# Moving twelve small matrix products from the end of one expert stage into the next, and the routing steps around them

## The reference, cut to what matters

```python
# fourth: mixture of 8 experts, 2 per token (also run as the sixth)
gate_logits = xt @ Wg.T + bg
w, idx = top_k(gate_logits, 2); w = softmax(w)
h = relu(xt @ W1[e].T + b1[e]); y = h @ W2[e].T + b2[e]      # per expert e
out = sum over the two chosen experts of w * y
x = x + 0.5 * out
# fifth: attention over 256 fixed source rows, 16 heads of 64
v = (value_embedding @ Wv + bv).reshape(256, 16, 64)
ctx = softmax(qn @ kn.T / 8) @ v;   h = ctx @ Wo + bo
```

## Time and profile before

| | |
|---|---|
| three runs, us | 1052.39, 1052.88, 1051.32 (median 1052.39) |
| profiled execution, us | 1052.39 |
| its span, first to last instruction, us | 1050.6 |
| mean granted TensorE clock | 0.827 |
| D1 on TensorE | about 555 to 606 us |
| D2 on TensorE | about 606 to 651 us |
| S2 on TensorE | from 651.25 us |

### The profile page before, as it was taken

The page is one execution under the profiler, slowest core; times in us unless marked ns, Lnnn a source line. Parts: engine busy times, 40 slices in busy tenths (PEclk is TensorE's granted clock), DMA queues, the critical chain, the costliest instruction groups (busy, mean ns, idle before and its releaser), DMA issues.

```text
span 1050.6 us, 18271 instructions
## 1 busy us (share of the span) xinstructions
PE 946.2 (90%) x5092; PEld 725.6 (69%) x5092; DVE 789.6 (75%) x3092; ACT 576.1 (55%) x1313; POOL 459.1 (44%) x538
## 2 busy tenths in 40 slices
PE   5999988998889898966999999989999999997994
PEld 2668866877677676755996677866666666667863
DVE  5865899999999999995556963547878786866234
ACT  3547654554544454523764554867767677652541
POOL 2620079887568767845003762013602040132034
PEclk9999965555555555555999999999999999998998
DMA  9976422000700000022675315630100000005852
GB/s 305 315 230 200 129 72 100 14 13 11 102 2 13 8 1 9 14 75 82 203 215 168 100 49 161 185 104 21 42 1 1 1 22 1 1 24 168 248 161 73
DMA packets 63444, 95.66 MB, mean 91 GB/s; under 512 B 12128, under 2 KB 41968, under 8 KB 63216
## 3 DMA queue, kind: packets, MB, share of 16 engines
q1 hardware_dynamic: 46256, 71.94, 23.6%
q0 software_dynamic: 6144, 12.60, 4.2%
q10 hardware_dynamic: 10944, 9.97, 2.8%
HBM read 69.94 MB, written 30.83 MB: 96 GB/s over the span
## 4 chain that ended last, share of the span: by engine, by line
PE 45%; DVE 26%; issue 3%; ACT 3%; POOL 3%; DMA 1%; SPq 0%; POOLq 0%; ACTq 0%; DVEq 0%
DVE vb L1745 10%; PE bank L798 10%; DVE sg L1747 9%; PE bank L407 6%; PE bank L783 5%; PE bank L420 4%; PE bank L364 4%; PE bank L376 3%; PE bank L773 3%; PE bank L767 2%; PE bank L552 1%; PE bank L395 1%; POOL yg L2101 1%; PE bank L321 1%; PE bank L759 1%
## 5 line engine op out<-in xcount | busy, mean ns | idle before, releaser
L2101 POOL DMA_INDIRECT yg<-ys,posg x96 | 95.2, 992 | 140.7 <-issue 70.1
L1770 POOL TENSOR_SCALAR vb<-sS,vb 128x256 f32<-128x256 f32 x126 | 115.7, 930 | 67.7 <-DVE vb L1745 62.4
L1745 DVE MAX8 vb<-sg 128x8 f32<-128x256 f32 x384 | 142.6, 411 | 0.0
L1144 ACT ACTIVATE hb<-sS,negm 128x256 f32<-128x256 f32 x128 | 58.0, 502 | 115.3 <-POOL negm L2117 114.0
L2085 POOL DMA_INDIRECT xsc<-xnS,posu x96 | 96.3, 1003 | 53.3 <-DVE posu L1516 26.8
L407 PE MATMUL bank<-xbT,ws 128*128 128x256 f32 x456 | 114.3, 388 | 0.0
L552 PEld LDWEIGHTS bank<-kn,qn 128*128 128x128 f32 x512 | 112.0, 320 | 1.5 <-ACT qn L1150 1.5
L552 PE MATMUL bank<-kn,qn 128*128 128x17 f32 x512 | 106.5, 349 | 1.0 <-ACT qn L1150 1.0
L1747 DVE MATCH_REPLACE8 sg<-vb,sg 128x256 f32<-128x256 f32 x256 | 102.5, 406 | 0.0
L1776 POOL TENSOR_TENSOR hb<-vb,hb 128x512 f32<-128x512 f32 x63 | 79.9, 1269 | 31.5 <-ACT hb L1144 24.5
L364 PE MATMUL bank<-xnT,ws 128*128 128x512 f32 x192 | 92.7, 611 | 0.8 <-ACT xnT L958 0.8
(11 more groups left out here) (225 smaller groups left out, 1910.5 us busy)
## 6 DMA issues: line engine op xcount, KB each, us to landing
ws<-tab_m SPq DMA_DIRECT2D x46, 450.0 KB, 4.1
ws<-tab_m SPq DMA_DIRECT2D x54, 321.0 KB, 3.5
xb<-xsc SPq DMA_DIRECT2D x76, 128.0 KB, 3.2
ys<-ysb ACTq DMA_DIRECT2D x76, 128.0 KB, 3.4
xsc<-qn SPq DMA_DIRECT2D x3, 2048.0 KB, 16.3
pk<-packed SPq DMA_DIRECT2D x1, 3209.0 KB, 11.0
tab_m<-packed SPq DMA_DIRECT2D x5, 512.0 KB
ws<-packed SPq DMA_DIRECT2D x8, 256.0 KB, 4.4
```

The costliest lines, as they stand in the source:

```text
L1745: e.max(m8s[:, m:m + 8], s).then_inc(A["tk"], 1)
L1770: i = e.tensor_scalar(msk[:, n * S:n * S + S], sS[:, s:s + S], m[:, n, TOPK - 1:TOPK], None, ALU.is_ge)
L2101: e.indirect_dma_start(yg[:, y:y + D], None, ys[:, :], at(posg[g.p], g.order[t], k)).then_inc(s_g[t % GY], 16)
```

## The change

The twelve value steps all go into D2; the two that stood at steps 16 and 17 of D1 go to steps 1 and 2 of D2, and the later ones are spread anew. `D2.m` is transposed on TensorE before the last `pe_dense_second` of D1. In D2 the routing of p2 starts one step earlier on TensorE, but its place on VectorE comes one step later; that of p3 comes one to two steps later: its rank on TensorE goes from step 9 to step 11, and the transpose of the D2 weights from 10 to 11. On VectorE the four combines of D1's step 15 become one at step 14, one at 15 and two at 16. GpSimd scatters three tiles' halves, then five, then the rest, where it was four, three and the rest.

```diff
-        VALUES_D1 = {16: (0, 1), 17: (1, 1)}
-        VALUES_D2 = {4: (2, 0), 6: (3, 1), 7: (4, 1), 10: (5, 1), 11: (6, 1), 12: (7, 1), 13: (8, 1), 14: (9, 1), 15: (10, 1),
-                     16: (11, 1)}
+        VALUES_D2 = {1: (0, 0), 2: (1, 0), 3: (2, 0), 4: (3, 0), 6: (4, 0), 8: (5, 1), 9: (6, 1), 10: (7, 1),
+                     13: (8, 1), 14: (9, 1), 15: (10, 1), 16: (11, 1)}
...
             if n == 0:
                 e.wait_ge(s_ld[4], 16)
-                e.wait_ge(M["off"], S2.parts[0].nth)
-            elif n == 2:
                 e.wait_ge(R["lg"], D2.m.q + 1)
-            elif n == 3:
+            elif n == 5:
                 e.wait_ge(M["off"], S2.parts[1].nth)
-            elif n == 5:
+            elif n == 8:
                 e.wait_ge(M["off"], S2.parts[2].nth)
...
             elif j == 16:
-                pe_values(e, *VALUES_D1[j])
-            elif j == 17:
                 e.wait_ge(F["b2x"], D1.i + 1)
                 pe_T(e, D2.m)
-                pe_values(e, *VALUES_D1[j])
+            elif j == 17:
                 pe_logits(e, D2.m)
...
-            if j == 3:
-                values_read(e, 2)
+            if j == 2:
+                e.wait_ge(M["off"], p1.nth)
                 pe_T(e, p2)
-            elif j == 4:
+            elif j == 3:
                 pe_logits(e, p2)
             elif j == 5:
                 pe_rank_part(e, p2)
-            elif j == 6:
-                values_read(e, 3)
+            elif j == 7:
+                values_read(e, 5)
                 pe_T(e, p3)
-            elif j == 7:
+            elif j == 9:
                 pe_logits(e, p3)
-            elif j == 9:
-                values_read(e, 5)
+            elif j == 11:
+                e.wait_ge(M["off"], p2.nth)
+                values_read(e, 8)
                 pe_rank_part(e, p3)
-            elif j == 10:
-                e.wait_ge(R["lg"], p3.q + 1)
                 pe_combT(e, D2)
-            elif j == 11:
+            elif j == 12:
                 pe_b2(e, D2)
...
-        COMBINE_D1 = {5: (0,), 6: (1,), 7: (2,), 8: (3,), 9: (4,), 10: (5,), 11: (6,), 12: (7,), 15: (8, 9, 10, 11)}
+        COMBINE_D1 = {5: (0,), 6: (1,), 7: (2,), 8: (3,), 9: (4,), 10: (5,), 11: (6,), 12: (7,), 14: (8,), 15: (9,), 16: (10, 11)}
...
-            elif j == 15:
+            elif j == 16:
                 dve_stats(e, p2)
+            elif j == 18:
+                dve_top2(e, D2.m)
...
             if j == 0:
                 dve_stats(e, p3)
-                dve_top2(e, D2.m)
...
-            elif j == 7:
+            elif j == 9:
                 dve_top2(e, p3)
-            elif j == 8:
+            elif j == 10:
                 dve_choice(e, p3)
-            elif j == 9:
+            elif j == 11:
                 dve_place_part(e, p3)
                 dve_place_end(e, S2)
...
-            pool_scatter(e, S2, 0, 4)
+            pool_scatter(e, S2, 0, 3)
             pool_rstd(e, S2.parts[1])
-            pool_scatter(e, S2, 4, 7)
+            pool_scatter(e, S2, 3, 2 * CT)
             pool_rstd(e, S2.parts[2])
-            pool_scatter(e, S2, 7)
+            pool_scatter(e, S2, 2 * CT)
```

More of the change, by code:

```diff
@@ L727, in values_read, with pe_values @@
             after(e, C["VOe"], n - 4)
-        def pe_values(e, n, b):
+        def pe_values(e, j):
+            n, b = VALUES_D2[j]
             if n == 0:
                 e.wait_ge(s_ld[4], 16)
-                e.wait_ge(M["off"], S2.parts[0].nth)
-            elif n == 2:
                 e.wait_ge(R["lg"], D2.m.q + 1)
-            elif n == 3:
+            elif n == 5:
                 e.wait_ge(M["off"], S2.parts[1].nth)
-            elif n == 5:
+            elif n == 8:
                 e.wait_ge(M["off"], S2.parts[2].nth)
@@ L887, in pe_beside_d2 @@
                 pe_rank_part(e, p2)
-            elif j == 6:
-                values_read(e, 3)
+            elif j == 7:
+                values_read(e, 5)
                 pe_T(e, p3)
-            elif j == 7:
+            elif j == 9:
                 pe_logits(e, p3)
-            elif j == 9:
-                values_read(e, 5)
+            elif j == 11:
+                e.wait_ge(M["off"], p2.nth)
+                values_read(e, 8)
                 pe_rank_part(e, p3)
-            elif j == 10:
-                e.wait_ge(R["lg"], p3.q + 1)
                 pe_combT(e, D2)
-            elif j == 11:
+            elif j == 12:
                 pe_b2(e, D2)
             if j in VALUES_D2:
-                pe_values(e, *VALUES_D2[j])
+                pe_values(e, j)
         def pe_beside_s2(e, n):
@@ L945, in tensor_program @@
             pe_dense(e, D2, pe_beside_d2)
-            values_read(e, len(VALUES_D1) + len(VALUES_D2))
+            values_read(e, len(VALUES_D2))
             pe_blocks(e, S2, pe_beside_s2)
@@ L1264, in act_a1_key, with act_values @@
                 act_a1_sq(e, key_step(j, 1))
-        def act_values(e, n, b):
+        def act_values(e, j):
+            n, b = VALUES_D2[j]
             if n == 0:
@@ L1324, in act_beside_d1 @@
                 act_xn(e, D2.m)
-                act_values(e, *VALUES_D1[16])
                 act_xnT(e, D2.m)
-                act_values(e, *VALUES_D1[17])
         def act_beside_d2(e, j):
@@ L1332, in act_beside_d2 @@
                 act_xn(e, p2)
-            elif j == 2:
+            if j in VALUES_D2:
+                act_values(e, j)
+            if j == 2:
+                act_th(e, D2.m)
                 act_xnT(e, p2)
[L1335 to L1340, removed]
+            elif j == 4:
                 act_th(e, p2)
             elif j == 6:
+                act_xn(e, p3)
+            elif j == 7:
                 act_xnT(e, p3)
-            elif j == 8:
+            elif j == 10:
                 act_th(e, p3)
-            elif j == 10:
+            elif j == 11:
                 act_combT(e, D2)
@@ L1381, in scalar_program @@
             act_dense(e, D2, act_beside_d2)
-            act_values(e, *VALUES_D2[2 * E])
+            act_values(e, 2 * E)
             e.preload_act_table_set("natural_log_exp_and_others")
@@ L2002, in dve_beside_d2 @@
                 dve_choice(e, p2)
+            elif j == 5:
                 dve_place_part(e, p2)
-            elif j == 7:
+            elif j == 9:
                 dve_top2(e, p3)
-            elif j == 8:
+            elif j == 10:
                 dve_choice(e, p3)
-            elif j == 9:
+            elif j == 11:
                 dve_place_part(e, p3)
```

## The result

Four runs of the changed kernel took 1057.31 to 1060.13 us, median 1058.88 us; four runs of the kernel before, on the same chip, 1051.32 to 1052.88 us, median 1052.62 us. The ratio is 1.0058, with a 95% interval of 1.0044 to 1.0072: slower by about 6 us. Forecast were 1056.3 us, in a range from 1052.6 to 1058.4 us. The record has nine more executions of the changed kernel, the profiled one among them, without runs of the kernel before set beside them; all thirteen lie between 1056.54 and 1060.50 us, with a median of 1058.00 us.

What follows compares the result with a forecast made beforehand. TensorE, busy 90% of the span, was taken as the bound, with VectorE pacing D1's end. D1's gain -0.65, value steps +1.74, new D2 waits +1.15 and clock +1.7 gave +3.94 us on 1052.39: 1056.3 us, range 1052.6 to 1058.4.

Steps and rivals of the forecast that it cites:

- the term of 1.7 us for the fall of the clock: Behind TensorE's longer pause at D1's end the clock falls to half rate, losing 1.7 us of full-speed work.
- The upper bound of the term: A second clock fall, for the 0.8 us wait in D2, would cost another 1.7 us; not expected.
- x(5) 0.65 us later: End of D1: tile 8's combine ahead of x(5) on VectorE delays it and the last second product, to 602.39.
- Transpose of `D2.m` inside the pause, at about 600.9: End of D1: the transpose falls into TensorE's wait before the last second product, taking 0.44 us off the path.
- VT0 and VT1 cost 1.74 us in D2: Early D2: the two moved value steps add 2 x 0.87 us on TensorE, which had no gap there.
- Waits of 0.8 and 0.25 us in D2: Early D2: TensorE waits 0.8 us for p2's normalised rows before its transpose, 0.25 us before VT1 for bank 0.
- VO7's 0.78 us stays: In D2, TensorE's existing 0.78 us wait before VO7, for the eviction of VO6, remains.
- The first block: S2's first block lands at 651.9 to 653.0, before TensorE comes at 653.49, so it stays hidden; cover 0.5 us.
- What follows S2 moves as a whole: After S2 the work keeps its order and shifts together; nothing counted for it.
- the clock stays up: Rival, end of D1: the transpose in the pause is enough to hold the clock; +2.24 us, 1054.6 us, chance 0.20.
- waits are covered: Rival, D1's end and early D2: x(5) not later, no new waits, clock stays; +0.44 us, 1052.8 us, chance 0.10.
- The other side: Rival, D1's end: x(5) done before TensorE's transpose, all three old waits saved, 2.83 us; 1049.6 us, chance 0.10.

Runs made afterwards that it cites:

- combines back: The changed kernel with the four combines of tiles 8 to 11 back at VectorE's step 15, behind x(5): 1054.45 us, ratio 1.0032.
- two value steps back: The changed kernel with VT0 and VT1 back at steps 16 and 17 of D1, all else as changed: 1054.42 us, ratio 1.0025.
- useless work in D1: The changed kernel with four extra matmuls, results never read, in TensorE's pause before the transpose of D2.m: 1055.38 us against 1052.33 us, ratio 1.0035.
- logits behind wide products: The changed kernel with the logits of D2.m moved behind the first two products of D2: 1056.45 us, ratio 1.0043.
- value steps alone, second run: The kernel before with only VT0 and VT1 moved from D1 to steps 1 and 2 of D2, repeated on another chip: 1057.26 us against 1051.63 us.
- x(5) early, second run: The kernel before with x(5) ahead of p1's place, VT0 and VO7 on bank 0, repeated on another chip: 1049.76 us against 1051.63 us, ratio 0.9978.
- the experiment with useless work: The kernel before with useless matmuls in its two other long TensorE pauses, second attention and D3: 1052.52 us against 1051.63 us, ratio 1.0008.

## Why the prediction was right and wrong

The direction was right, and so was the kind of mechanism: a fall of the clock behind the longer pause. The size was not, and the median fell 0.5 us outside the range.

The step that failed is the term of 1.7 us for the fall of the clock in the sum -0.65 + 1.74 + 1.15 + 1.7. It measured 4.4 us: the clock was at half rate for 10.2 us and not for 3.4. The upper bound of the term, two times 1.7 us, lay below it too, and its reason did not occur: the wait of 0.41 us that was left brought no fall. With the rows, the sum is about 2.5 us without the clock, less 0.2 us of a shorter wait, plus 4.4: 6.7 us, as S2's start shows.

I had read the length from one pause of one trace and taken it for a constant. It is none, even with the same work on both sides. Eight profiles have this pause near 950 us, of 3.86 to 3.88 us for `zacc`, with the same 32 instructions behind it:

| kernel | 32 instructions start | clock falls, about | low clock, us |
|---|---|---|---|
| before | 953.22 | 954.1 | 3.4 |
| changed | 959.70 | 960.1 | 3.4 |
| combines back | 955.77 | 956.0 | 3.4 |
| two value steps back | 954.74 | 956.0 | 3.4 |
| useless work in D1 | 956.64 | 955.6 | 6.8 |
| logits behind wide products | 957.37 | 956.3 | 6.8 |
| value steps alone, second run | 960.03 | 958.3 | 6.8 |
| x(5) early, second run | 950.04 | 948.9 | 6.8 |

Two rows of the fifth:

```profile
955.00:956.00 1.00, 0.00 (x0) 0.82 0.19 66
...
956.64 6.61 PE L796 MATMUL bank<-VO,sS 128*128 128x129 f32 x32 [3.88 <-DVE zacc L1877]
```

Where the clock fell after TensorE had gone back to work it stayed low for 3.4 us, where it fell before that for 6.8. The same pause has both, so its length and the work behind it do not fix the cost. Nor is the moment of the fall a rule for D1: with the value steps alone it fell behind the restart and stayed low for 10.2 us. The trace of before held a warning. For 100 us in another stage the clock is near half rate, with TensorE busy for 91 of them:

```profile
200.00:300.00 100.00, 91.35 (x385) 0.52 0.21 34
```

With this row in view the term would have had a wider bound. That the forecast missed by so little is partly luck: the term was short by 2.7 us, and the time grew by less than S2's start moved.

- *x(5) 0.65 us later*: x(5) started 0.66 us later, the last second product at 602.40 where 602.39 was forecast. The kernel with the combines back undid this.
- *Transpose of `D2.m` inside the pause, at about 600.9*: 600.93. That it would not keep the clock up was called likelier than not, and so it was in all profiles with the transpose alone.
- *VT0 and VT1 cost 1.74 us in D2*: not measured alone. The part without the clock came to 2.5 us, for 2.24 by the sum of the three terms.
- *Waits of 0.8 and 0.25 us in D2*: 0.61 us for p2's transpose where the clock stayed up (useless work in the pause), 0.41 us where it fell, as TensorE came later. VT1 waits for nothing in these rows.
- *VO7's 0.78 us stays*: 0.78.
- *The first block*: the way from p3's rank to SyncE's first request was 13.04 us, forecast 1.57 + 8.85 + 2.54 = 12.96. There was no wait for `xb`. Rank and request came some 2.5 us later than the latest value named; with the clock up (useless work in D1) the rank stood at 637.39, for 636.97 by the sum.
- *What follows S2 moves as a whole*: nearly. The low clock near 954 us differs from one execution to the next; the experiment with useless work shows no cost of it in the time. What the second spell, near 961 us at the start of S3, costs was not measured.
- The rivals "the clock stays up" and "waits are covered" were not what happened; the kernel with two value steps back has the clock up and gave 1.0025, near the first one's +2.24 us, but by other waits, so this is no proof of it. "The other side" was wrong here, but its place was right: the kernel with x(5) early is faster, with the last second product 0.70 us and S2 2.04 us earlier.

What stays open: why the clock stayed low for 10.2 us here and not for 3.4 or 6.8. The four runs of the changed kernel spread over 2.8 us, those of before over 1.6 us; a low clock whose length varies from one execution to the next would do that, but only one execution of each was profiled.

## What to carry to other kernels

Before moving small work out of a wait of TensorE, ask what else it does there: it may cost nothing where it stands and hold the clock up for everything behind it. Do not price a fall of the clock from one spell of one trace: give it a range, from the shortest spell to the longest that several traces show. Then ask whether TensorE is the path there: half rate cost 4.4 us at the start of D2, where TensorE hardly waits, and nothing that the time shows before S3, where something else sets the start. And to shorten such a wait, move what the other engine does ahead of the release, here p1's place behind x(5), rather than filling the wait.

## What was not expected of the hardware

- At the end of D1 the low clock lasted 3.4 us (combines back), 6.8 us (logits behind wide products) and 10.2 us (the changed kernel, and the value steps alone), with TensorE busy nearly all through it. Behind the pause near 950 us it lasted 3.4 us four times and 6.8 us four times, with the same work.
- The clock fell once behind a wait of only 0.78 us (at 651.9 us in the kernel with useless work in D1), in a stretch of value steps that use 64 of the 128 rows; in the other profiles shown here the same wait at the same place brought no fall. And in the kernel with x(5) early a pause of 3.09 us in D3 brought none, where one of 3.04 us at this place did in the kernel before. Waiting time alone does not foretell it:

```profile
1035.62 2.02 PE L376 MATMUL bank<-ws,hb 128*128 128x128 f32 x16 [3.09 <-DVE x L1595]
```

- The section "Part 1: The HAM clock gate" of the Trainium skill's "TensorE: Matmul & The Clock Gate" says that idleness brings the clock down and activity releases it. The traces agree on the fall behind most pauses of 3.0 to 3.9 us, with or without 0.4 us of transposes in them, but not behind the one of 3.09 us above. On the release they agree less: from 200 to 300 us TensorE is busy for 91 us by the trace, and the clock is at 0.52.
